# Linear attention on one core: turned scores copied by ScalarE without a mask, the mask of the diagonal blocks moved to the first small product's copy, one table load ahead of the root

## The reference, cut to what matters

```python
def _step(S, xs):
    qt, kt, vt, gt, bt = xs
    S = S * jnp.exp(gt)[..., None, None]
    pred = jnp.einsum('bhk,bhkv->bhv', kt, S)
    delta = (vt - pred) * bt[..., None]
    S = S + jnp.einsum('bhk,bhv->bhkv', kt, delta)
    return (S, jnp.einsum('bhk,bhkv->bhv', qt, S))
...
q = l2norm(q) * dk ** (-0.5)
k = l2norm(k)
```

## Time and profile before

| | |
|---|---|
| median of 3 runs | 1227.35 us |
| lowest, highest | 1223.6, 1232.17 us |
| profiled execution, device time | 1228.41 us |
| its span in the trace | 1226.7 us |
| mean granted TensorE clock | 0.927 of full speed |
| third stage, within the span | some 777 to 1168 us |

### The profile page before, as it was taken

How to read it: one execution, slowest core, us unless ns; L and a number is a source line. 1 busy time by engine, 2 the same in 40 slices (tenths; PEclk the granted TensorE clock), 3 DMA queues, 4 the chain that set the end, 5 groups by cost and what they waited for, 6 DMA issues and landing times. The chain is left out here.

```text
span 1226.7 us, 26372 instructions
## 1 busy us (share of the span) xinstructions
PE 1124.7 (92%) x9980; PEld 963.5 (79%) x9980; DVE 852.9 (70%) x2427; ACT 637.3 (52%) x1596; POOL 211.1 (17%) x245
## 2 busy tenths in 40 slices
PE   3999999999999998999999999578799889898888
PEld 2799899889989987888888898456577667776767
DVE  4677567647856776667766757798889779777343
ACT  4654444444444443553444434456788688665341
POOL 0422132222222222430000000200220121021100
PEclk9999999999999998999999999678798798867789
DMA  9020000000000003001000000100000000000034
GB/s 311 2 70 2 1 1 1 1 1 1 2 1 1 1 1 95 1 1 28 1 1 1 1 1 30 57 30 3 32 30 3 31 31 30 3 2 3 25 94 141
DMA packets 26701, 32.90 MB, mean 27 GB/s; under 512 B 4960, under 2 KB 21968, under 8 KB 26576
## 3 DMA queue, kind: packets, MB, share of 16 engines
q1 hardware_dynamic: 24400, 29.12, 7.5%
q10 hardware_dynamic: 2176, 2.10, 0.5%
HBM read 29.04 MB, written 2.17 MB: 25 GB/s over the span
## 5 line engine op out<-in xcount | busy, mean ns | idle before, releaser
L365 DVE TENSOR_TENSOR a_ps<-a_ps,causal 128x256 f32<-128x256 f32 x128 | 54.7, 427 | 100.9 <-PE a_ps L635 100.9
L1537 PE MATMUL b_ps<-ln_high,b_high 128*128 128x512 f32 x256 | 101.6, 397 | 1.0 <-ACT gate_up_raw L1452 1.0
L683 PE MATMUL a_ps<-a_wo_high,a_oT 128*128 128x256 f32 x512 | 101.2, 282 | 0.1
L1537 PE MATMUL b_ps<-ln_low,b_high 128*128 128x512 f32 x256 | 100.8, 394 | 0.0
L1537 PE MATMUL b_ps<-ln_high,b_low 128*128 128x512 f32 x256 | 100.5, 392 | 0.0
L348 POOL TENSOR_TENSOR a_probs<-a_probs,a_inv 128x256 f32<-128x256 f32 x64 | 40.2, 627 | 339.9 <-DVE a_inv L385 339.9
L1571 PE MATMUL b_ps<-b_wd_high,b_mid 128*128 128x256 f32 x512 | 97.8, 286 | 0.0
L508 ACT ACTIVATE a_probs<-a_ps,a_negmax 128x128 f32<-128x128 f32 x128 | 47.1, 368 | 88.8 <-DVE a_negmax L371 79.5
L520 ACT CAST a_oT<-a_ps 128x512 fp32r<-128x512 f32 x64 | 37.5, 587 | 107.1 <-PE a_ps L661 107.1
L1452 ACT ACTIVATE gate_up_raw<-b_ps 128x512 f32<-128x512 f32 x64 | 37.4, 597 | 101.4 <-PE b_ps L1537 101.3
L1337 DVE TENSOR_TENSOR gate_up_raw<-gate_up_raw,b_ps 128x512 f32<-128x512 f32 x64 | 42.8, 685 | 62.8 <-ACT gate_up_raw L1452 34.2
(11 more groups left out here) (438 smaller groups left out, 3101.9 us busy)
## 6 DMA issues: line engine op xcount, KB each, us to landing
gate_up_raw<-a_scratch SPq DMA_DIRECT2D x8, 768.0 KB, 3.6
d_main<-in_D_main SPq DMA_DIRECT2D x14, 304.5 KB
x<-in_hidden SPq DMA_DIRECT2D x4, 512.0 KB, 10.6
a_raw<-in_A_q SPq DMA_DIRECT2D x4, 512.0 KB, 8.3
gate_up_raw<-in_A_o SPq DMA_DIRECT2D x1, 2048.0 KB
gate_up_raw<-in_B_g SPq DMA_DIRECT2D x1, 2048.0 KB, 12.2
gate_up_raw<-in_B_u SPq DMA_DIRECT2D x1, 2048.0 KB, 8.3
out<-x ACTq DMA_DIRECT2D x8, 256.0 KB, 2.2
```

Source lines behind the costliest of these rows:

```text
L365: nc.vector.tensor_tensor(diagonals, diagonals, r.causal[:].rearrange("p (o k) -> p o k", o=1).to_broadcast([P, 2, P]), ALU.add).then_inc( ...
L683: mm = nc.tensor.matmul(ps[:, out_bank(job), 0:HID], opart, wpart, start=(k == 0 and j == 0), stop=(k == QUARTER - 1 and j == len(passes) ...
L1537: mm = nc.tensor.matmul(ps[:, bank, :], wpart, xpart, start=(j == 0), stop=(j == len(passes) - 1))
```

## The change

`off_diagonal` is gone from VectorE, and with it the mask. ScalarE gets `copy_low`: the same three banks, copied as they are, two of them behind `place_off` and the third between `square_of(c, 1)` and `squares(s, 0)`. The diagonal blocks of 16, which `low` now holds, would enter only the first small product. They are kept out there: `copy_part16` takes only the right half of each pair's columns and multiplies the rows by `sides[:, 0:1]`, which is 1 on the rows of even blocks and 0 on the others; the rest of `part16` is zeroed once at the start on GpSimd. In `root`, a table that holds both Ln and Exp is loaded by name ahead of Ln.

```diff
@@ delta, gpsimd
                 for block_rows in (firstT, secondT):
                     nc.gpsimd.memset(block_rows[:], 0.0)
+                nc.gpsimd.memset(part16[:], 0.0)
                 nc.gpsimd.memset(first[:], 0.0).then_inc(S["cleared"], 1)
@@ delta, vector
-                def off_diagonal(m, p):
-                    dve.wait_ge(S["lT_ready"], at("lT_ready", m, p + 1))
-                    nc.vector.tensor_tensor(low[:, m % 2, p * 2 * HALVES:(p + 1) * 2 * HALVES, :],
-                                            ps[:, L_BANKS[p], :].rearrange("p (t k) -> p t k", k=P),
-                                            off_blocks[:].to_broadcast([P, 2 * HALVES, P]), ALU.mult
-                                            ).then_inc(S["l_ready"], 1)
...
-                    wide = kept.blocks.rearrange("p (b o) -> p b o", o=1).to_broadcast([P, BLOCKS, SUB])
-                    nc.vector.tensor_scalar(off_blocks[:, 0, :].rearrange("p (b t) -> p b t", b=BLOCKS), wide,
-                                            -1.0, 1.0, ALU.mult, ALU.add)
...
                     run(c, scan, 2)
-                    run(m, off_diagonal, 0)
                     run(m, fold_odd)
-                    run(m, off_diagonal, 1)
                     run(m, shuffles)
...
                     run(m, column_sum, 7)
-                    run(m, off_diagonal, 2)
                     run(m, column_product, 8)
@@ delta, scalar
+                def copy_low(m, p):
+                    act.wait_ge(S["lT_ready"], at("lT_ready", m, p + 1))
+                    nc.scalar.copy(low[:, m % 2, p * 2 * HALVES:(p + 1) * 2 * HALVES, :].rearrange("p u k -> p (u k)"),
+                                   ps[:, L_BANKS[p], :]).then_inc(S["l_ready"], 1)
+
                 def copy_part16(b):
+
+                    if b == 0:
+                        act.wait_ge(S["cleared"], at("cleared", 0, 1))
+                        act.wait_ge(consts, 1)
                     act.wait_ge(S["pa_ready"], at("pa_ready", b, 1))
-                    nc.scalar.copy(flat(part16[:]), ps[:, PART16_BANK, 0:WIDE32]).then_inc(S["pa_copied"], 1)
+                    nc.scalar.activation(part16[:, :, SUB:], ps[:, PART16_BANK, 0:WIDE32].rearrange(
+                        "p (u t) -> p u t", u=UNITS)[:, :, SUB:], ACT.Copy, scale=sides[:, 0:1]
+                                         ).then_inc(S["pa_copied"], 1)
...
                 def root(d):
                     act.wait_ge(S["summed"], at("summed", d, HALVES))
+                    nc.scalar.preload_act_table_set("natural_log_exp_and_others")
                     nc.scalar.activation(ms[:], ms[:], ACT.Ln, bias=eps[:], scale=1.0 / DV).then_inc(S["root_ready"], 1)
...
                     run(s, place_off)
+                    run(m, copy_low, 0)
+                    run(m, copy_low, 1)
                     run(m, values_by_token, 0)
...
                     run(c, square_of, 1)
+                    run(m, copy_low, 2)
                     run(s, squares, 0)
```

More of the change, by code:

```diff
@@ L817, in __init__ @@
         self.last_zeros = view(PRODUCT + DC * VALS, P)
-        self.off_blocks = view(PRODUCT + DC * VALS + P, 1, P)
         self.a_all = view(SPREAD, DH, SEQ)
@@ L1930, in delta @@
                                                       kept.eps)
-        off_blocks, head_ones, chan, square, a_all, g_all = (kept.off_blocks, kept.head_ones, kept.chan, kept.square,
-                                                             kept.a_all, kept.g_all)
+        head_ones, chan, square, a_all, g_all = kept.head_ones, kept.chan, kept.square, kept.a_all, kept.g_all
         even_neg, odd_neg = sb("even_neg", [P, 1]), sb("odd_neg", [P, 1])
```

## The result

| | before | after |
|---|---|---|
| median, us | 1225.47 (4 runs, 1215.77 to 1232.17) | 1210.44 (4 runs, 1206.98 to 1213.33) |
| ratio after / before | | 0.9899, 95% interval 0.9858 to 0.9940 |
| profiled execution (span), us | 1228.41 (1226.7) | 1213.33 (1211.6) |
| mean granted TensorE clock | 0.927 | 0.939 |
| third stage in the profile, us | 391.4 | 379.8 |

The account below looks back on a forecast made before the run. TensorE, then VectorE, then both in turn were taken to bound a round. Gains of 1.34 (round 0), 0.31 (round 1), 0.55 (rounds 2 to 6) and 1.0 (rounds 7, 8), 3.2 us, gave 1224.2 us; range 1214 to 1230.

Parts of the forecast that it names:

- The step that failed: ScalarE's third copy moves the norm roots by 0.35 us; GpSimd and VectorE take results later, so no cost.
- Nothing is removed in the rest of the round: Rounds 2 to 6, behind `second_values`: no further gain beyond the 0.11 us a round ahead of it.
- rival C: Jobs behind `add_out` run at TensorE's upper clock, 5 x 1.6 = 8 us gained, 1216 us; chance 0.08.
- Rounds 2 to 6 up to `second_values`: `second_values` starts only 0.11 us sooner, when `known` ends: 5 x 0.11 = 0.55 us gained.
- rival A: VectorE bounds the round after all; all 24 x 0.6 count, 15.7 us with the load, 1211.7 us; chance 0.10.
- Round 0: VectorE has no pause there; removed calls give 0.14 and twice 0.6, 1.34 us gained.
- Round 1: `second_values` can start when `known` ends, 0.31 us sooner than before.
- `root`: Rounds 7 and 8: second table load goes, last batch's `pair_inverses` starts 1.4 us sooner; 1.0 us gained together.
- the first two copies on ScalarE: They take 0.54 us each and fall into ScalarE's pauses in rounds 2 to 6; taken as nothing.
- D: The third copy makes `copy_wkT` late for `known`: 7 x 0.54 = 3.8 us against 3.2, 1228 us; chance 0.12.
- the memset: GpSimd's new 128x384 memset costs 0.42 us ahead of `decayed_keys(0)`, hidden before its results are needed; taken as nothing.
- B: TensorE's first stretch drops to the lower clock in five middle rounds: 9 us slower, 1236 us; chance 0.05.

Follow-up runs that it names:

- run 6: Kernel before, with one idle ScalarE instruction (`square_of(c, 1)` done twice) where the change puts the third copy: 1215.97 us, ratio 0.9940.
- run 2: Kernel before, with GpSimd's `queries` held until VectorE has finished column product 12: 1223.3 us, ratio 1.0014.
- Runs 3: Changed kernel with the third copy back on VectorE at its old place, unmasked: 1220.63 us, ratio 0.9990 to the kernel before.
- run 12: Kernel before, with only the table load by name ahead of Ln in `root` added: 1220.60 us, ratio 0.9986.
- run 9: Changed kernel again, unchanged, measured beside another version on the same chip: 1207.72 us, ratio 0.9882 to the kernel before.
- run 4: Changed kernel with the first two copies back on VectorE, unmasked, the third still on ScalarE: 1212.42 us, ratio 0.9907 to the kernel before.
- runs 7: Changed kernel without the table load by name in `root`: 1213.65 us, ratio 0.9931 to the kernel before.
- run 11: Kernel before, with only GpSimd's `decayed_keys` held until column product 13 is done: 1209.69 us, ratio 0.9882.

## Why the prediction was wrong

**The step that failed** is the one that took ScalarE's shift as nothing: "It also moves the norm roots by 0.35 behind a pause of 0.19 at the taps; GpSimd and VectorE take their results 0.4 us and over 1 us later, ahead of a full VectorE." I asked whether anyone would wait for a late result, and nobody does. I didn't ask what GpSimd's instruction would then run beside. A shift of 0.16 us, with product 12 itself 0.05 us sooner, put it behind product 12 instead of ahead of it. Runs 6 and 2 show that step by itself, once with and once without a gain.

**With it fell** "Nothing is removed in the rest of the round": 0.44 us were, in each of rounds 2 to 6, 2.2 us in all, and the argument against rival C, "that pause stays, as `add_out` keeps its place". Rival C, with its chance of 0.08, had the right kind of gain: the jobs behind the turns at the upper level of the clock. That its price came out is in part luck: it counted five times 1.6 us, 8 in all; measured are four turns, of 2 us each. And it named nothing that would shorten the pause. Its rows stood in the prediction, a pause of 1.52 us and jobs of 3.52, without the question how near to the edge 1.52 is. Runs 3 and 12, with 1.51 to 1.53, show both outcomes.

**The other terms.** Rounds 2 to 6 up to `second_values`: 0.07 us each instead of 0.11. `keep_state` waits 1.41, 1.42, 1.39, 0.31 and 0.42 us in them, before 0.30, 0.65, 1.13, 0.30 and 0.53. In rounds 5 and 6, then, it waits no longer while the rounds are shorter, which I had named as the sign of rival A; but in the second profile of the changed kernel (run 9) it waits 1.06 to 1.41 in all five, as forecast. What refutes A is run 4, with two of three copies still on VectorE and nearly the whole gain. Round 0: 49.36 to 48.45 in the first two profiles, 0.9 for 1.34; over the profiles with three masked copies on VectorE it takes 48.9 to 49.8, over those with none 46.9 to 48.5, so about 2 us. Round 1: 0.31 is not visible, as that round varied from 46.8 to 52.7 us. Together with the turns: 8 + 2.2 + 2 + 0.35 = 12.6 of the 13 to 17 us in the medians. The 8 hold for a kernel before with all four turns low, as in its one profile. At the same pause, 1.51 to 1.53 us, only 7 of 12 turns were low; an average execution would then gain some 5 at the turns by this estimate, and the sum would be 9 to 10.

**`root`**: forecast 1.0; the first two profiles show next to nothing, and the times of runs 7 and 12 can't size it. `pair_inverses` did start sooner, its wait is 1.85 instead of 2.75 us, but the work behind it gave it back. The end of L2749 (L2748 before) waits, in the timelines of before and after:

```profile
1131.88 0.43 PE L2748 MATMUL c_ps<-cb_inv32T,cb_low 32*32 32x32 f32 x9 [0.50 <-issue]
```

```profile
1111.35 1.61 PE L2735 MATMUL c_ps<-cb_part,cb_inv 32*32 32x32 f32 x96 [1.85 <-issue]
...
1116.26 0.43 PE L2749 MATMUL c_ps<-cb_inv32T,cb_low 32*32 32x32 f32 x9 [1.15 <-issue]
```

Counted from that round's transpose (1123.93 and 1108.46) these last products start at 7.95 and 7.80 us, and the round takes 44.84 and 44.98. In these two the 0.9 us were worth nothing in length, 0.15 at these products. What the last nine products wait for the trace calls issue; it stays open. Over all 14 profiles that round, up to the fourth stage's table load, took 43.1 to 45.0 us with the load by name in `root` (eight, mean 44.0) and 43.9 to 45.6 without it (six, mean 44.8). So the forecast 1.0 may be about right in the mean; it is not shown.

**Rightly taken as nothing**: the first two copies on ScalarE (0.59 us each), the third in front of `copy_wkT` (D: the new wait of `second_values` is for `known`, 0.32, and `copy_wkT` is not late for it), the memset. The sign that I named for B or C, a clock of the first stretch that differs by more than 0.05, stayed silent: the 16.2 us ahead of `second_values` have 0.87 to 0.90 before and 0.86 to 0.91 after in rounds 2 to 6. I looked at the clock in the wrong place: what differs is the turn, 0.66 to 1.00.

**What stays open.** That the pause at the turns decides between the two groups of medians is shown; that the turns are all of the gain is not. Run 6 took 1216.0 and run 11 1209.7 with the same pauses and the same clock in the turns. Run 4, with all four turns at 1.00, took 163.7 us for rounds 3 to 6, where the changed kernel took 158.6, and run 12, with a low turn and pauses of 1.51, took 164.2; run 4's clock over these rounds is 0.87 to 0.88. Its second stretch at the lower level is the longer one, and no run here changes that stretch alone. Over whole executions the clock's median is 0.929 in the kernel before and 0.942 in run 9 beside it. By the formula above that is some 33 us less at the lower level, of which four turns hold 13. Among the 17 executions of that kernel before, those with the lower clock are the longer ones (0.923 and 1230.2 us, 0.938 and 1216.2 us). And 3.7 us of the 15.1 between the two profiles lie ahead of the stage, in code that is the same; in the other twelve profiles the stage starts at 772.2 to 776.0 us, so the first profile (777.36) was a late one.

## What to carry to other kernels

When work is moved from one engine to another, list what the moved instructions now run beside, not only who waits for them. If a VectorE instruction with two SBUF inputs starts within a tenth or two of one on GpSimd, the order can tip, and 0.45 us goes one way or the other. Where TensorE's clock stands at the lower level behind a pause, that pause is worth more than its length: here 0.5 us less of it gave 2 us more at each turn that had been low, and a single wait on GpSimd, which shortened it, gave as much as the whole change.

## What the runs showed of the hardware that I had not expected

- A pause of 0.99 to 1.06 us left the clock at 2.4 GHz in all 24 turns, one of 1.67 to 1.69 in none of four, one of 1.51 to 1.53 in 5 of 12. Of run 2's four, 1.56 to 1.58 left it there in one of three, and 1.78 did in the one case, so above 1.5 us the length of the pause alone does not settle it.
- Round 7 has two lengths, whatever the kernel: 31.7 to 34.6 us in nine profiles with a clock of 0.75 to 0.90, and 37.5 to 39.0 in five with 0.65 to 0.73. The same kernel shows both, in the first profile after and in run 9:

```profile
1070.46:1108.46 38.00, 34.25 (x603) 28.09 (x602) 22.23 (x83) 20.76 (x45) 3.10 (x2) 0.73 0.01 3
```

```profile
1068.61:1101.63 33.02, 29.03 (x603) 23.39 (x602) 22.24 (x82) 20.40 (x45) 3.11 (x2) 0.84 0.01 3
```

  These 5 us are as much as a good part of what separates runs of one kernel (1216 to 1232 before), and neither version controls them.
- An added ScalarE instruction made the kernel 8 us faster (run 6).
